# Cross attention in fp32 quality on TensorE: V in two fp16 pieces with a per-batch scale, and one tile in eight split on GpSimd

## The reference

```
Q = (x @ Wq + bq);  K = (c @ Wk + bk);  V = (c @ Wv + bv)        # 512 -> 1024, heads of 64
scores = (Q K^T) / 8 * mask                                       # the mask multiplies
attn = softmax(scores)
out = (attn V) @ Wo + bo
y = x + out;  layernorm(y, eps 1e-5) * gamma + beta
```

## Time and profile before

| | |
|---|---|
| time, median of 3 runs | 2552.56 us (2549.45 to 2553.84) |
| the profiled execution: its time, its span | 2553.46 us, 2551.9 us |
| TensorE busy | 2477.4 us, 97% of the span |
| VectorE, ScalarE, GpSimd busy | 2031.9, 1806.0, 1284.3 us (80%, 71%, 50%) |
| granted TensorE clock, mean | 0.990 of full |
| DMA, share of 16 engines' time | 79.0% in the queue that carries almost all |
| instructions | 50788 |

### The profile page before, as it was taken

The page is one execution under the profiler, slowest core; times in us unless marked ns, Lnnn a source line. Parts: engine busy times, 40 slices in busy tenths (PEclk is TensorE's granted clock), DMA queues, the critical chain, the costliest instruction groups (busy, mean ns, idle before and its releaser), DMA issues.

```text
span 2551.9 us, 50788 instructions
## 1 busy us (share of the span) xinstructions
PE 2477.4 (97%) x14336; PEld 1676.5 (66%) x14336; DVE 2031.9 (80%) x4128; ACT 1806.0 (71%) x3809; POOL 1284.3 (50%) x1671
## 2 busy tenths in 40 slices
PE   5999999999999999999899999999999999999995
PEld 4566666666666666666566666666666666666663
DVE  4778787878877878877787888888888888888884
ACT  4777677777776767777677777777777777777773
POOL 2455344455344555344453565655565655565644
PEclk9999999999999999999999999999999999999997
DMA  5978778778788788788888877877888877877864
GB/s 143 183 167 186 169 172 189 176 177 179 169 179 187 174 182 177 163 186 181 186 175 185 186 176 178 182 176 165 187 177 176 185 175 163 188 176 176 189 140 113
DMA packets 1165326, 446.05 MB, mean 175 GB/s; under 512 B 1078881, under 2 KB 1078881, under 8 KB 1165281
## 3 DMA queue, kind: packets, MB, share of 16 engines
q1 hardware_dynamic: 1161728, 444.70, 79.0%
q10 hardware_dynamic: 3552, 0.80, 0.2%
HBM read 143.41 MB, written 33.55 MB: 69 GB/s over the span
## 4 chain that ended last, share of the span: by engine, by line
PE 95%; DVE 2%; DMA 1%; POOL 1%; SPq 1%; ACT 0%; issue 0%; POOLq 0%; DVEq 0%; ACTq 0%
PE ctx_ps L407 22%; PE fill_ps L336 20%; PE fill_ps L337 18%; PE fill_ps L338 18%; PE score_ps L384 7%; PE score_ps L387 5%; PE score_ps L390 5%; DVE score_ps L656 1%; DVE p L672 0%; SPq L220 0%; DMA raw<-in_ct 0%; DMA raw<-in_L_xattn_Wo 0%; DVE wq_lo L646 0%; DMA raw<-in_xt 0%; ACT probs L502 0%
## 5 line engine op out<-in xcount | busy, mean ns | idle before, releaser
L672 DVE SCALAR_TENSOR_TENSOR p<-probs,inv_sum,p 128x512 f16<-128x512 f32 x1024 | 873.8, 885 | 29.4 <-ACT p L515 25.7
L502 ACT ACTIVATE probs<-score_ps,neg_max 128x512 f32<-128x512 f32 x1024 | 694.8, 684 | 245.7 <-POOL neg_max L860 220.8
L656 DVE CUSTOM_DVE_ANT_0 score_ps<-score_ps,mask_sb 128x512 f32<-128x512 f32 x1024 | 692.1, 706 | 160.5 <-PE score_ps L390 158.5
L515 ACT ACTIVATE p<-probs,inv_sum 128x512 f16<-128x512 f32 x1024 | 682.2, 715 | 186.8 <-DVE inv_sum L665 186.6
L407 PE MATMUL ctx_ps<-pT,v 128*64 128x512 f16 x5120 | 584.0, 383 | 20.9 <-POOL v L891 10.3
L860 POOL TENSOR_SCALAR neg_max<-row_max 128x2 f32<-128x2 f32 x512 | 234.5, 458 | 701.9 <-DVE row_max L656 701.6
L407 PEld LDWEIGHTS ctx_ps<-pT,v 128*64 128x64 bf16 x5120 | 283.2, 111 | 307.1 <-issue 75.0
L867 POOL TENSOR_SCALAR down_sum<-row_sum 128x4 f32<-128x4 f32 x256 | 50.3, 197 | 463.5 <-ACT probs L502 456.9
L384 PE MATMUL score_ps<-k_hi,q_hi 64*128 64x512 f32 x1024 | 244.9, 469 | 5.7 <-ACT probs L502 5.7
L336 PE MATMUL fill_ps<-xT_hi,wq_hi 128*128 128x512 f32 x512 | 208.2, 407 | 23.3 <-DVE wq_lo L646 22.9
L336 PE MATMUL fill_ps<-wv_hi,cT_hi 128*128 128x512 f32 x512 | 211.1, 412 | 0.4 <-issue 0.3
(11 more groups left out here) (60 smaller groups left out, 4074.5 us busy)
## 6 DMA issues: line engine op xcount, KB each, us to landing
raw<-in_xt SPq DMA_DIRECT2D x128, 256.0 KB, 3.3
raw<-in_ct SPq DMA_DIRECT2D x128, 256.0 KB, 3.4
mask_sb<-in_mask_Bx1xSxS_fk SPq DMA_DIRECT2D x128, 256.0 KB, 3.2
acc<-in_x SPq DMA_DIRECT2D x64, 256.0 KB, 3.4
partial<-acc SPq DMA_DIRECT2D x64, 256.0 KB, 3.0
acc<-partial SPq DMA_DIRECT2D x64, 256.0 KB, 3.0
out<-acc SPq DMA_DIRECT2D x64, 256.0 KB, 2.1
pT<-p SPq DMA_TRANSPOSE x512, 4.5
```

Of the source, the lines that this page charges most:

```text
L502: nc.scalar.activation(probs[:, i % E_TILES, :], score_ps[:, i % 4, :], ACT.Exp, bias=neg_max[:, p % 2, i:i + 1], accum_out=row_sum[:, p % ...
L515: nc.scalar.activation(p16[:, q, a, 0, :], probs[:, i % E_TILES, :], ACT.Copy, scale=inv_sum[:, p % 2, i:i + 1]).then_inc(p_rounded, 1)
L656: nc.vector.tensor_tensor_reduce(out=score_ps[:, i % 4, :], in0=score_ps[:, i % 4, :], in1=mask_sb[:, q, :], scale=SCORE_SCALE, scalar=-3. ...
L672: nc.vector.scalar_tensor_tensor(out=p16[:, q, a, 1, :], in0=probs[:, i % E_TILES, :], scalar=inv_sum[:, p % 2, i:i + 1], in1=p16[:, q, a, ...
```

## The change

V is held in two fp16 pieces instead of three bf16 ones, and `PIECES` has three products instead of five. fp16 has a narrow range, so V is scaled per step. VectorE takes the maximum absolute value of each row of the transposed context (`input_maximum`, 4 a step on 128x512) and of Wv (once a group), multiplies and sums them per partition (`bound_products`); one small matmul with one output column sums over the partitions into `ctx_ps` (`bound_inputs`); VectorE turns that into the scale (`value_scale`) and the factor that undoes it (`undo_scale`), GpSimd scales bv (`scale_bias`). The scale is used where V is rounded and split, and undone where the output projection is added to `acc`. `split_value` on GpSimd is gone; V's second piece is written by VectorE straight into its place.

`E_TILES` goes from 4 to 8, and tile 7 of each pair gets its fp16 difference from GpSimd by two instructions (`split_probs` of the gpsimd block, which is in the code of before and not used by it).

All five bodies have another order, and `FILL_BANK` another assignment. TensorE's and the start of SP's are shown; those of the other three engines are cut to what is new in them.

```diff
-E_TILES = 4
-POOL_TILES = ()
+E_TILES = 8
+POOL_TILES = (7,)
-PIECES = ((0, 0), (0, 1), (0, 2), (1, 0), (1, 1))
+PIECES = ((0, 0), (0, 1), (1, 0))
+BOUND_DOWN = 1.0 / 16384.0
+BOUND_FLOOR = 1.0e-30
-FILL_BANK = dict(zip("O2 O3 Q0 Q1 K0 K1 V0 V1 Q2 K2 Q3 V2 V3 O0 K3 O1".split(),
+FILL_BANK = dict(zip("O2 O3 Q0 Q1 K0 K1 K2 Q2 V0 V1 Q3 K3 V2 O0 V3 O1".split(),
                      (0, 1, 2, 0, 1, 2, 0, 1, 2, 0, 1, 2, 0, 1, 2, 1)))
-        v_piece = [sb(f"v{i}", [P, KT, GW], BF16) for i in range(3)]
-        v_rest = sb("v_rest", [P, 2, GW])
+        v_piece = [sb(f"v{i}", [P, KT, GW], F16) for i in range(2)]
...
 # sync: body
                 if nxt:
                     load_input(nxt, "x", range(0, 1))
                 if here:
-                    transpose_probs(here, 1, range(1, 2))
-                if nxt:
-                    load_input(nxt, "c", range(0, 1))
+                    transpose_probs(here, 0, range(3, 4))
+                if nxt:
                     load_input(nxt, "x", range(1, 3))
...
 # tensor
+            def bound_inputs(at):
+                g, b, n = at
+                pe.wait_ge(bound_multiplied, n + 1)
+                if isinstance(n, int) and n == 0:
+                    pe.wait_ge(consts_set, 4)
+                else:
+                    pe.wait_ge(ctx_split, (n - 1) * PAIRS + 3)
+                nc.tensor.matmul(ctx_ps[:, 0:1], bound_part[:, 0:1].to_broadcast([P, P]), ones, start=True, stop=True).then_inc(
+                    bound_summed, 1)
...
                 if here:
                     scores(here, 2, range(3, 4))
+                    scores(here, 3, range(0, 1))
                     values(here, 0)
-                    scores(here, 3, range(0, 2))
                 if prev:
                     fill(prev, "O", 3)
+                if here:
+                    scores(here, 3, range(1, 2))
                 if nxt:
                     fill(nxt, "Q", 0)
+                if here:
+                    scores(here, 3, range(2, 3))
+                if nxt:
                     fill(nxt, "Q", 1)
-                if here:
-                    scores(here, 3, range(2, 4))
+                    fill(nxt, "K", 0)
+                if here:
+                    scores(here, 3, range(3, 4))
                     values(here, 1)
                 if nxt:
-                    fill(nxt, "K", 0)
+                    scores(nxt, 0, range(0, 1))
                     fill(nxt, "K", 1)
-                    scores(nxt, 0, range(0, 2))
+                    scores(nxt, 0, range(1, 2))
+                    fill(nxt, "K", 2)
                 if here:
                     values(here, 2)
                 if nxt:
-                    scores(nxt, 0, range(2, 3))
+                    scores(nxt, 0, range(2, 4))
+                    fill(nxt, "Q", 2)
                     fill(nxt, "V", 0)
-                    scores(nxt, 0, range(3, 4))
+                    bound_inputs(nxt)
+                    scores(nxt, 1, range(0, 2))
                     fill(nxt, "V", 1)
-                    scores(nxt, 1, range(0, 1))
                 if here:
                     values(here, 3)
                 if nxt:
-                    scores(nxt, 1, range(1, 2))
-                    fill(nxt, "Q", 2)
-                    fill(nxt, "K", 2)
                     scores(nxt, 1, range(2, 3))
                     fill(nxt, "Q", 3)
                     scores(nxt, 1, range(3, 4))
+                    fill(nxt, "K", 3)
                     fill(nxt, "V", 2)
+                    scores(nxt, 2, range(0, 1))
+                if here:
+                    fill(here, "O", 0)
+                if nxt:
+                    scores(nxt, 2, range(1, 2))
                     fill(nxt, "V", 3)
-                    scores(nxt, 2, range(0, 2))
-                if here:
-                    fill(here, "O", 0)
-                if nxt:
-                    fill(nxt, "K", 3)
                     scores(nxt, 2, range(2, 3))
                 if here:
                     fill(here, "O", 1)
...
 # vector
+                if w == "v":
+                    ...
+                    nc.vector.tensor_reduce(wv_max[:, quarter:quarter + 1], raw_weight(w, quarter), AXIS.X, ALU.max,
+                                            apply_absolute_value=True).then_inc(wv_max_taken, 1)
...
+            def input_maximum(at, tiles):
+                    ...
+                    nc.vector.tensor_reduce(c_max[:, i:i + 1], raw_input("c", i), AXIS.X, ALU.max,
+                                            apply_absolute_value=True).then_inc(c_max_taken, 1)
+
+            def bound_products(at):
+                ...
+                nc.vector.tensor_tensor_reduce(
+                    out=bound_part[:, 1:5], in0=c_max[:, :], in1=wv_max[:, :], scale=1.0, scalar=0.0,
+                    op0=ALU.mult, op1=ALU.add, accum_out=bound_part[:, 0:1]).then_inc(bound_multiplied, 1)
+
+            def value_scale(at):
+                ...
+                nc.vector.tensor_scalar(bound, ctx_ps[:, 0:1], BOUND_DOWN, BOUND_FLOOR, ALU.mult,
+                                        ALU.max).then_inc(bound_ready, 1)
+                dve.wait_ge(bound_ready, n + 1)
+                nc.vector.reciprocal(v_scale, bound).then_inc(scale_ready, 1)
+
+            def undo_scale(at):
+                ...
+                nc.vector.tensor_scalar(undo, bound, P_DOWN, 1.0, ALU.mult,
+                                        ALU.mult).then_inc(undo_ready, 1)
...
-                    if not (isinstance(n, int) and n == 0 and k < 2):
-                        dve.wait_ge(v_split, n * KT + k - 1)
                     nc.vector.scalar_tensor_tensor(
-                        out=v_rest[:, k % 2, :], in0=bank, scalar=P_DOWN, in1=v_piece[0][:, k, :],
-                        op0=ALU.mult, op1=ALU.subtract).then_inc(v_rest_done, 1)
+                        out=v_piece[1][:, k, :], in0=bank, scalar=v_scale, in1=v_piece[0][:, k, :],
+                        op0=ALU.mult, op1=ALU.subtract).then_inc(v_split, 1)
...
-                    nc.vector.tensor_tensor(acc[:, k, :], bank, acc[:, k, :], ALU.add).then_inc(acc_added, 1)
+                    nc.vector.scalar_tensor_tensor(
+                        out=acc[:, k, :], in0=bank, scalar=undo, in1=acc[:, k, :],
+                        op0=ALU.mult, op1=ALU.add).then_inc(acc_added, 1)
...
 # gpsimd
-            def split_value(at, tiles):
-                ...
+            def scale_bias(at):
+                ...
+                nc.gpsimd.tensor_scalar(bv_scaled, bias_col["v"][:, cols], v_scale, P_UP, ALU.mult,
+                                        ALU.mult).then_inc(bias_scaled, 1)
...
 # gpsimd: body
                 if here:
                     scale_sums(here, 2, 0)
-                    split_value(here, range(3, 4))
-                    negate_max(here, 2, range(2, 3))
+                    split_probs(here, 1, range(7, 8))
...
+                if here:
+                    split_probs(here, 3, range(7, 8))
                 if nxt:
                     negate_max(nxt, 0, range(3, 4))
```

More of the change, by code:

```diff
@@ L414, in body @@
                     users.update((FILL_BANK[f"{kind}{k}"], fill_read(before + ahead, kind, k))
-                                 for kind, k, ahead in (("V", 3, 1), ("O", 1, 0), ("K", 3, 1)))
+                                 for kind, k, ahead in (("V", 2, 1), ("O", 1, 0), ("V", 3, 1)))
                 if prev:
@@ L542, in body @@
                 if here:
[L543 to L544 removed]
+                    exponentials(here, 2, range(5, 6))
+                    round_probs(here, 2, range(0, 2))
                 if nxt:
@@ L678, in split_context @@
                 dve.wait_ge(ctx_rounded, n * PAIRS + p + 1)
-                col = g * PAIRS + p
+                if p == 0:
+                    dve.wait_ge(bias_scaled, n + 1)
                 nc.vector.scalar_tensor_tensor(
-                    out=ctx_lo[:, p, :], in0=ctx_ps[:, :], scalar=bias_col["v"][:, col:col + 1], in1=ctx_hi[:, p, :],
+                    out=ctx_lo[:, p, :], in0=ctx_ps[:, :], scalar=bv_scaled[:, p:p + 1], in1=ctx_hi[:, p, :],
                     op0=ALU.add, op1=ALU.subtract).then_inc(ctx_split, 1)
+            def input_maximum(at, tiles):
+                g, b, n = at
+                for i in tiles:
+                    if i == 0 and not (isinstance(n, int) and n == 0):
+                        wait_alone(dve, bound_multiplied, n)
+                    wait_alone(dve, xc_in[DT + i], (n + 1) * DMA)
+                    nc.vector.tensor_reduce(c_max[:, i:i + 1], raw_input("c", i), AXIS.X, ALU.max,
+                                            apply_absolute_value=True).then_inc(c_max_taken, 1)
@@ L757, in body @@
                 if here:
+                    mask_and_max(here, 3, range(3, 4))
+                    split_probs(here, 2, range(3, 4))
+                    mask_and_max(here, 3, range(4, 5))
+                if nxt:
+                    evacuate(nxt, "Q", 0)
+                if here:
```

(16 more changed lines are left out.)

427 lines of the change are left out of this document (240 added, 187 removed).

## The result

The changed kernel takes 2380.89 us (median of 4 runs, 2379.22 to 2382.33) against 2552.14 for the kernel before on the same chip: a ratio of 0.933, 95% interval 0.9314 to 0.9346. The forecast was 2388. The profiled execution took 2381.32 us, with a span of 2379.5.

A forecast was written before the change was run, and what follows sets the result against it. TensorE was taken to bound every full step, VectorE next. 2553.5 - 217 + 25 + 13 + 4 = 2378 us if TensorE never waits, +10 for short waits: 2388 us; range 2355 to 2440.

The forecast's parts named there:

- `values` calls: TensorE's `values` calls go from 20 to 12 pairs of matmuls, losing 1.70 us each: -217 us over 128 calls.
- changes of kind: TensorE's new order has four more switches between fills, scores and `values` a body, 0.20 us each: +25 us.
- small matmul: One-column fp32 matmul on TensorE's path, taken at 0.4 us a step: +13 us.
- ends: Maxima ahead of the first weight splits (+3 us) and at start and group change (+1 or so): +4 us.
- waits in full steps: Short TensorE waits expected as VectorE's slack shrinks to 6.8 us: 0.3 us a step, +10 us.
- bound from below: The one-column matmul costs nothing if it slips into the change from fill to scores behind which it stands.
- rival A: VectorE's strict list comes too late, needing 8.4 us of slack: step 72.9 us, +50, 2428 us; chance 0.20.
- upper bound of 1.27: VectorE's four context maxima, stretched beside GpSimd's work to 1.27 us each, would make 66.9 us a step.
- B: The DMAs bound: if their busy share can't pass 0.85, step 72.9 us, near 2428 us; chance 0.08.
- thin cover of `values(0)`: Transposes pass behind the next body's input loads, with only 3 steps of TensorE work before the `values` wanting them.
- Rival C: Waits long enough to lower TensorE's clock, fills 0.43 us apart: 3.6 us a step, 2490 us; chance 0.05.
- Rival D: GpSimd's tile split ahead of `negate_max` delays the score loop: step 80.1 us, 2651 us, slower than before; chance 0.04.

The follow-up runs named there:

- experiment 1: The changed kernel with five products again (two on operands that do not belong in the sum, for time only): 2594.23 us, ratio 1.0158.
- Experiment 9: The changed kernel with a constant V scale of 1/16384; maxima, small matmul, scale, its undoing and scaled bias left out: 2368.98 us, ratio 0.9283.
- experiment 6: The changed kernel with four extra VectorE maxima a step, of a constant row, placed where VectorE stood idle: 2381.88 us, ratio 0.9322.
- experiment 3: The kernel before, in its own order, with three products, eight probs buffers and no V work on GpSimd: 2417.62 us, ratio 0.9464.
- experiment 5: The changed kernel with each context maximum taken twice, the extra one right ahead of the first: 2424.00 us, ratio 0.9487.
- experiment 10: The old order with three products and eight buffers, two waiting score blocks moved in TensorE's list: 2553.44 us, ratio 0.9993.
- experiment 4: The changed kernel with tile 7 of each pair split on VectorE instead of GpSimd: 2391.10 us, ratio 0.936.
- experiments 2: The kernel before with only `PIECES` changed, to three products: 2422.65 us, ratio 0.9496.
- experiment 8: The changed kernel with `scores(1, 3)` behind `scores(1, 2)`, its exponential and negate_max moved earlier: 2368.56 us; maxima behind the Wq split too: 2370.03 us.
- experiment 7: The changed kernel with `scores(1, 3)` right behind `scores(1, 2)`: 2385.70 us; with `scores(2, 1)` also ahead of O0: 2417.46 us.

## Why the prediction was right

The mechanism was as told: TensorE's work sets the time, and nothing came up from below. That nothing would was assumed in the sum and not worked out, and there the prediction had luck (the old order, below). The terms of the sum, from the profiled executions:

| term | forecast | measured |
|---|---|---|
| `values` calls, 128 | -217 | -220 (1.72 each; experiment 1: -213 in time) |
| changes of kind | +25 (0.20) | +25 to +27 (0.20 to 0.22) |
| small matmul | +13 (0.4) | +4 (0.12) |
| ends | +4 | +11.5 |
| waits in full steps | +10 | 0 |
| longer fills, cause open | | +7.6 (0.25 x 31) at 0.20 a change |
| sum | -165 | -172 |

- **Ends.** +11.5 is the 4.6 found above and the 6.9 that the four calls outside the 31 steps gave back. Experiment 9 shows 9.7 of it to be the scale's. I had costed the start at +3 and "+1 or so" for the rest: the term was too small by a factor of three. That an instruction counts in full where TensorE already waits is my reading of it, not shown.
- **Small matmul.** The bound from below was nearer. Of the four passes that the Trainium skill ("FP8 and Floating Point Precision", on fp32) has for true FP32, the profile has two matmul records and two loads for each (64 for 32), and 0.12 us in the chain.
- **Short waits.** The 0.3 us a step were a hedge between the sum and rival A. The trace has none. This term and the small matmul were 10 and 9 us too high; the ends and the fills, 7.5 and 7.6 us too low, took most of that back, so that 2388 came out only 7 high. That closeness is partly luck.
- **VectorE and GpSimd.** 64.5 was forecast and 63.99 is there; the maximum at 0.675 was costed at 0.68 and the sum into `acc` at 0.744 (0.741). The maxima are not stretched beside GpSimd (668 to 687 ns in all 128), so the upper bound of 1.27 fell. That agrees with what the prediction took from the Trainium skill, "GPSIMD Engine Reference" and "VectorE: DVE Perf Modes". V's second piece was costed like `v_rest` (0.687) and takes 0.745. GpSimd's tile split is 0.841 + 1.317 us for 0.845 + 1.364; its busy time is 44.2 a step for 45.3.
- **DMA.** A share of 0.87 was forecast from a fixed amount of full load, 62 us a step. It is 0.80, and 0.88 in experiment 6 at the same rate of 192 GB/s. The share is no amount of work, and B was built on taking it for one. The thin cover of `values(0)` held: TensorE waits for pT once, in the last part. V's type costs nothing, as assumed: a call takes 2.71 us with bf16 pieces (experiment 3, 629.51) as with fp16.
- **Rival A** is refuted as it was put. VectorE kept 7.2 us of slack in the changed kernel, below the 8.4 that A needed, and 4.9 in experiment 6 (744.87 of 800 us, so 66.3 of 71.2), without a wait. But its mechanism, VectorE's list too late at one place, is real: experiment 5 with nearly the same sum costs 43 us. What A lacked was the place.
- **Rival C** didn't come in the changed kernel. Its mechanism came in experiment 10, in the steps that I read, and in two of fourteen steps of experiment 5.
- **Rival D** fell by the time itself and by experiment 4, in which the kernel without the tile on GpSimd is slower.
- **The old order.** By experiments 2 and 3 the kernel with the products alone would be at 2418 to 2423. The changed order, the scale's 12 us paid, is at 2391 without the GpSimd tile and 2381 with it. So the order is worth some 38 us (2417.6 - 2391.1 + 11.9, by difference; the kernel that would show it alone wasn't run). The prediction charged it 25 us for changes and named no gain. Its working applied to the old order, 2553.5 - 217 = 2336 us, would have missed by more than 80 us. It was right because the sum took "if TensorE never waits" for given, with 10 us for short waits, and the new order is what makes it so.

Open: why some fills of the new order take 0.05 to 0.1 us longer, when a short wait brings the lower clock, and what the old order would do mended at its two places. Four buffers with the new order weren't tried, since by my reading its lists would wait for each other.

## What to carry to other kernels

When the bound engine's work shrinks, look not only for the next engine by its sum, but for every block that the removed work was covering: a call that gets 1.7 us shorter can uncover the bank behind it, and a block that waits for it can cost TensorE twice the idle time that the profile shows. The slack to ask for is that between one instruction and the one which waits for it; a busy share of 93% cost nothing where each piece stood in a gap, and the same four maxima in the wrong place cost 2.3 us in most steps of group 1. Where a reorder saves a change of kind, move the loop that feeds the moved block (maximum, negation, exponential) with it, as experiment 8 did.

## What the runs showed of the hardware

- A change between fills, scores and `values` on TensorE costs 0.20 to 0.22 us (0.43 for two in experiment 7). "TensorEngine Tiling (Array Packing)" of the Trainium skill, in its key properties, has a change of tiling mode drain the engine and gives no price.
- TensorE's clock fell to 1.2 GHz behind single waits of 2.9 us (experiment 10, three steps read), and behind waits of 0.43 and 0.69 us in two of fourteen steps (experiment 5), while it stayed at full speed behind the same waits in the others.
- A block of scores whose two halves were released one after the other cost TensorE 1.14 us more with 0.59 us of idle time (experiment 3) and 1.65 more with 1.10 (experiment 5).
- A VectorE maximum of 128x512 fp32 takes 0.675 us and is not lengthened by GpSimd's work, while the subtraction with two SBUF inputs has a mean of 857 ns now and 885 before.
- A one-column fp32 matmul with a stationary operand of full width costs the array 0.12 us, between a fill and scores.
- The DMAs' busy share of the same transfers lay between 0.79 and 0.88 in steps of 71.15 to 71.27 us, at 192 to 194 GB/s.
